# Flamingo block, two layers, one core: the way from the inputs to the first loop of maxima, reordered

## The reference, cut to what matters

```
x = x + tanh(g_xattn[0]) * attention0(layernorm(x), ctx, ctx)
x = x + tanh(g_ffn[0])   * experts0(layernorm(x))          # 8 experts, top 2, gelu
x = x + tanh(g_xattn[1]) * attention1(ctx, ctx, layernorm(x), mask)
x = x + tanh(g_ffn[1])   * experts1(layernorm(x))          # 8 experts, top 2, silu gate
attention: q = x Wq + bq; k = ctx Wk + bk; v = ctx Wv + bv
           out = softmax(q k^T / sqrt(8)) v, per head; then Wo, bo
```

## Time and profile before

| | us |
|---|---|
| median of 3 runs | 2752.51 (2747.73 to 2755.5) |
| the profiled execution | 2751.86 |
| its span | 2749.9 |
| PE busy | 2538.1 (92%) |
| DVE busy | 2161.0 (79%) |
| ACT busy | 1939.8 (71%) |
| POOL busy | 41.2 (1%) |
| mean granted TensorE clock | 0.942 |

### The profile page before, as it was taken

How to read it: one execution, slowest core, us unless ns; L and a number is a source line. 1 busy time by engine, 2 the same in 40 slices (tenths; PEclk the granted TensorE clock), 3 DMA queues, 4 the chain that set the end, 5 groups by cost and what they waited for, 6 DMA issues and landing times.

```text
span 2749.9 us, 55587 instructions
## 1 busy us (share of the span) xinstructions
PE 2538.1 (92%) x23426; PEld 1015.6 (37%) x23428; DVE 2161.0 (79%) x2210; ACT 1939.8 (71%) x3545; POOL 41.2 (1%) x28
## 2 busy tenths in 40 slices
PE   2389999999999999997893899999999999999979
PEld 1243333333333333344441333333333333333334
DVE  5479999999999999944434899999999999999235
ACT  2058888888888888874330288888888888888942
POOL 3000000000000000000010000000000000000000
PEclk8559999999999999998895699999999999999989
DMA  7120000000000000003101000000000000000010
GB/s 247 67 77 27 28 27 27 27 28 29 28 29 28 27 28 27 20 32 112 62 0 61 9 28 29 28 29 29 27 27 27 27 28 28 29 29 15 2 62 8
DMA packets 38627, 103.11 MB, mean 37 GB/s; under 512 B 4164, under 2 KB 14936, under 8 KB 38120
## 3 DMA queue, kind: packets, MB, share of 16 engines
q1 hardware_dynamic: 36936, 99.14, 9.8%
q10 hardware_dynamic: 1440, 0.40, 0.1%
HBM read 83.72 MB, written 15.80 MB: 36 GB/s over the span
## 4 chain that ended last, share of the span: by engine, by line
PE 67%; DVE 26%; DMA 3%; SPq 3%; issue 1%; ACT 1%; POOL 1%; DVEq 0%; ACTq 0%; POOLq 0%
DVE m_part L654 24%; PE ps L971 23%; PE ps L923 20%; PE ps L942 10%; PE ps L1069 4%; PE ps L1077 3%; PE ps L990 3%; SPq L294 2%; PE ps L883 1%; DMA q_parts<-probs 1%; PE ps L913 1%; SPq L303 1%; DMA probs<-in_mask_t 1%; PE ps L875 1%; DVE probs L610 1%
## 5 line engine op out<-in xcount | busy, mean ns | idle before, releaser
L654 DVE TENSOR_REDUCE m_part<-ps 128x2 f32<-128x1024 f32 (+1 forms) x1664 | 1933.9, 1183 | 239.3 <-PE ps L942 235.6
L492 ACT ACTIVATE probs<-ps 128x512 f32<-128x512 f32 (+1 forms) x3264 | 1763.8, 595 | 366.1 <-PE ps L923 254.1
L971 PE MATMUL ps<-probs,v_all 128*9 128x256 f32 x13056 | 1013.4, 382 | 1.5 <-ACT o_raw L472 0.5
L923 PE MATMUL ps<-q_ring,k_ring 35*128 35x512 f32 x3264 | 864.8, 498 | 0.6 <-ACT q_ring L481 0.4
L942 PE MATMUL ps<-k_ring,q_ring 33*128 33x512 f32 (+1 forms) x3328 | 726.8, 419 | 92.4 <-DVE m_part L654 36.2
L923 PEld LDWEIGHTS ps<-q_ring,k_ring 35*128 35x128 f32 x3264 | 343.1, 183 | 665.9 <-ACT probs L492 560.6
L942 PEld LDWEIGHTS ps<-k_ring,q_ring 33*128 33x128 f32 x3328 | 349.9, 194 | 175.3 <-DVE m_part L654 101.4
L971 PEld LDWEIGHTS ps<-probs,v_all 128*9 128x9 f32 x13056 | 194.1, 88 | 551.0 <-ACT probs L492 445.0
L990 PE MATMUL ps<-neg_i,zeros 128*9 128x256 bf16 x2664 | 115.3, 276 | 0.0
L675 DVE RECIPROCAL r_den<-ps 128x8 f32<-128x8 f32 x32 | 6.6, 207 | 121.4 <-PE ps L950 121.4
L789 DVE TENSOR_TENSOR probs<-probs,k_ring 128x512 f32<-128x512 f32 x64 | 43.6, 691 | 64.9 <-ACT probs L525 56.6
(11 more groups left out here) (121 smaller groups left out, 598.7 us busy)
## 6 DMA issues: line engine op xcount, KB each, us to landing
k_ring<-k_parts SPq DMA_DIRECT2D x384, 96.0 KB
k_ring<-k_parts SPq DMA_DIRECT2D x128, 112.2 KB
k_ring<-gate_rows SPq DMA_DIRECT2D x16, 512.0 KB, 7.4
probs<-in_mask_t SPq DMA_DIRECT2D x10, 640.0 KB, 4.5
k_parts<-probs SPq DMA_DIRECT2D x12, 512.0 KB, 3.1
k_parts<-big SPq DMA_DIRECT2D x12, 512.0 KB, 3.1
q_ring<-q_parts SPq DMA_DIRECT2D x128, 32.0 KB
big<-in_w SPq DMA_DIRECT2D x1, 2048.0 KB, 10.8
```

Of the source, the lines that this page charges most:

```text
L492: A(probs[0:k, n % PSLOTS, HALF * half:HALF * half + HALF], ps[0:k, e_bank(unit), :], ACT.Exp, scale=SCALE).then_inc(sem(f"exp_done{l}"), 1)
L654: V.tensor_reduce(m_part[:, h % 2, :, p, c], mx(n % 2)[:, :, 0:chunk_w[c]], AX.X, ALU.max).then_inc(sem(f"mx_done{l}"), 1)
L923: pe.matmul(bank, k_ring[row:row + ROWS_EXP, koff:koff + P], q_ring[row:row + ROWS_EXP, qoff:qoff + HALF], start=not masked, stop=True).th ...
L971: mm = pe.matmul(ps[32 * g:32 * g + VW, 7, 0:QGW], v_all[0:k, t, h, :], probs[0:k, n % PSLOTS, QGW * g:QGW * g + QGW], start=(t == 0), sto ...
```

## The change

- The ones come by DMA. GpSimd fills a small tile of 3 x 204 ones; SP writes the three rows of each half with one transfer that reads this tile 64 times over (`set_ones`). GpSimd's memsets of 32 rows go, in both layers. TensorE waits for the ones ahead of the first loop.
- Values are projected between keys: `values(0, c)` follows `keys(0, c)`, and ScalarE evacuates both in turn (`project_kv`). The first loop holds none.
- First keys group by group: SP stores three chunks, loads the queries of head 0, stores three more, loads group 0, stores three, loads group 1, and so on (`load_first0`). TensorE waits for all 13 splits ahead of the first loop, since the loop uses the same two banks.
- The mask is summed inside the heads: SP issues mask chunk h - 2 in its turn for head h, and ScalarE sums chunk h - 1 in step 12 of heads 1 to 11. The stage for it lies in another place (`sum_stage`).
- `total_mask` runs ahead of the key and value work of head 15.

```diff
+ONES_W = 204
+MASK_AT = 12
...
+        sum_stage = [spare[:, n * MCH * TQ // 4:(n + 1) * MCH * TQ // 4].bitcast(U8) for n in range(2)]
+        sum_junk = spare[:, 2 * MCH * TQ // 4:3 * MCH * TQ // 4].bitcast(BF16)
+        ones_at = ga_at + 6 * QT * E + 6 * QT
+        ones_w = spare[0:3, ones_at:ones_at + ONES_W]
-        RING_SET = 4 + 2 * KRING, 6 + 2 * KRING
+        RING_SET = 2 + 2 * KRING
+        ONES_IN = 2 * 16
...
-            def store_k(l):
-                for c in range(NCH):
+            def store_k(l, c0=0, c1=NCH):
+                for c in range(c0, c1):
                     sp.wait_ge(sem(f"k_split{l}"), c + 1)
                     sp.dma_start(k_parts[l][:, :, HALF * c:HALF * c + chunk_w[c]],
                                  k_st[l][:, c % KST, :, 0:chunk_w[c]].bitcast(F32)).then_inc(sem(f"k_stored{l}_{c % KST}"), 16)
+
+            def set_ones(l):
+
+                sp.wait_ge(sem("ones_w"), 1)
+                if l:
+                    sp.wait_ge(sem("gated0"), 2 * E * 4)
+                wide = KRING * KW
+                for row in (KR, HB + KR):
+                    sp.dma_start(k_ring[row:row + 3, 0:wide].bitcast(F32).rearrange("p (n w) -> p n w", w=ONES_W),
+                                 ones_w[:, :].rearrange("p (o w) -> p o w", o=1).broadcast_to([3, wide // ONES_W, ONES_W])
+                                 ).then_inc(sem("ones_in"), 16)
 
             def store_q(l):
                 for half in range(2):
                     sp.wait_ge(sem(f"q_split{l}"), half + 1)
                     sp.dma_start(q_parts[l][:, :, HALF * half:HALF * half + HALF], q_st[:, half, :, :].bitcast(F32)).then_inc(sem(f"q_stored{l}"), 16)
 
-            def check_mask():
-                for c in range(NFULL // MCH):
-                    if c > 1:
-                        sp.wait_ge(sem("mask_summed"), c - 1)
-                    sp.dma_start(mask_stage[c % 2].rearrange("p (t q) -> p t q", q=TQ),
+            def check_mask(c):
+                if c > 1:
+                    sp.wait_ge(sem("mask_summed"), c - 1)
+                if c == 0:
+                    sp.wait_ge(sem("q_proj0"), 2)
+                if c < NFULL // MCH:
+                    sp.dma_start(sum_stage[c % 2].rearrange("p (t q) -> p t q", q=TQ),
                                  a["mask_t"][c * MCH * P:(c + 1) * MCH * P, :].rearrange("(t p) q -> p t q", p=P)
                                  ).then_inc(sem(f"mask_in{c % 2}"), 16)
-                sp.wait_ge(sem("mask_summed"), NFULL // MCH - 1)
-                sp.dma_start(mask_stage[0][0:TAIL, 0:TQ], a["mask_t"][NFULL * P:TK, :]).then_inc(sem("mask_in0"), 16)
+                else:
+                    sp.dma_start(sum_stage[c % 2][0:TAIL, 0:TQ], a["mask_t"][NFULL * P:TK, :]).then_inc(sem(f"mask_in{c % 2}"), 16)
...
                 sp.wait_ge(sem("ffn_done0"), 1)
+                sp.wait_ge(sem("ones_in"), 2 * ONES_IN)
...
-            def ready(l, what):
+            def ready(l, what, c1=NCH):
 
                 if what == "q":
                     sp.wait_ge(sem(f"q_stored{l}"), 16 * 2)
                 else:
                     for n in range(KST):
-                        sp.wait_ge(sem(f"k_stored{l}_{n}"), 16 * len(range(n, NCH, KST)))
-
-            def load_first(l):
-
-                sp.wait_ge(sem("ring_set"), RING_SET[l])
-                ready(l, "k")
-                if l:
-                    for g in range(len(K_GROUPS)):
-                        load_keys(l, 0, g)
-                    store_q(l)
-                ready(l, "q")
-                load_queries(l, 0)
-                if l == 0:
-                    for g in range(len(K_GROUPS)):
-                        load_keys(l, 0, g)
-                load_queries(l, 1)
+                        sp.wait_ge(sem(f"k_stored{l}_{n}"), 16 * len(range(n, c1, KST)))
+
+            def load_first0():
+
+                sp.wait_ge(sem("ring_set"), RING_SET)
+                for g, (c0, c1) in enumerate(K_GROUPS):
+                    if g == 0:
+                        store_k(0, 0, c1)
+                        ready(0, "q")
+                        load_queries(0, 0)
+                    if g + 1 < len(K_GROUPS):
+                        store_k(0, *K_GROUPS[g + 1])
+                    ready(0, "k", c1)
+                    load_keys(0, 0, g)
+                load_queries(0, 1)
                 for g in range(len(K_GROUPS)):
-                    load_keys(l, 1, g)
-                load_queries(l, 2)
+                    load_keys(0, 1, g)
+                load_queries(0, 2)
+
+            def load_first1():
+
+                set_ones(1)
+                ready(1, "k")
+                for g in range(len(K_GROUPS)):
+                    load_keys(1, 0, g)
+                store_q(1)
+                ready(1, "q")
+                load_queries(1, 0)
+                load_queries(1, 1)
+                for g in range(len(K_GROUPS)):
+                    load_keys(1, 1, g)
+                load_queries(1, 2)
...
                 for h in range(KRING, H):
+                    if l == 0 and h - KRING <= NFULL // MCH:
+                        check_mask(h - KRING)
...
             setup()
+            set_ones(0)
             store_q(0)
-            store_k(0)
-            load_first(0)
-            check_mask()
+            load_first0()
             load_heads(0)
...
             spread_gates(0)
-            load_first(1)
+            load_first1()
...
-            def set_ring(l):
-
-                wide = E * TQ if l else KRING * KW
-                if l:
-                    pool.wait_ge(sem("gated0"), 2 * E * 4)
-                cleared = []
-                if l == 0:
-                    cleared += [k_ring[row:row + 32, off + TK:off + KW] for row in (0, HB) for off in range(0, KRING * KW, KW)]
-                    cleared += [q_ring[row:row + 32, :] for row in (KR, HB + KR)]
+            def set_ring():
+
+                nc.gpsimd.memset(ones_w[:, :], 1.0).then_inc(sem("ones_w"), 1)
+                pool.wait_ge(sem("ones_w"), 1)
+                cleared = [k_ring[row:row + 32, off + TK:off + KW] for row in (0, HB) for off in range(0, KRING * KW, KW)]
+                cleared += [q_ring[row:row + 32, :] for row in (KR, HB + KR)]
                 for n, part in enumerate(cleared):
                     nc.gpsimd.memset(part.bitcast(F32), 0.0).then_inc(sem("ring_set"), 1)
                     pool.wait_ge(sem("ring_set"), n + 1)
-                for n, row in enumerate((KR, HB + KR)):
-                    nc.gpsimd.memset(k_ring[row:row + 32, 0:wide].bitcast(F32), 1.0).then_inc(sem("ring_set"), 1)
-                    pool.wait_ge(sem("ring_set"), RING_SET[l] - 1 + n)
...
-                set_ring(0)
+                set_ring()
...
             constants()
-            set_ring(1)
...
-            def project_k():
-                for c in range(NCH):
-                    w = chunk_w[c]
-                    act.wait_ge(sem("k_proj0"), c + 1)
-                    if c >= KST:
-                        act.wait_ge(sem(f"k_stored0_{c % KST}"), 16 * (c // KST))
-                    A(k_st[0][:, c % KST, 0, 0:w], ps[:, c % 2, 0:w], ACT.Identity, bias=b_col[:, 0, 1:2]).then_inc(sem("k_evac0"), 1)
...
+            def project_kv():
+                for c in range(NCH):
+                    w = chunk_w[c]
+                    act.wait_ge(sem("k_proj0"), c + 1)
+                    if c >= KST:
+                        act.wait_ge(sem(f"k_stored0_{c % KST}"), 16 * (c // KST))
+                    A(k_st[0][:, c % KST, 0, 0:w], ps[:, c % 2, 0:w], ACT.Identity, bias=b_col[:, 0, 1:2]).then_inc(sem("k_evac0"), 1)
+                    set_v(c)
...
-                A(mask_junk[0:rows, 0:n], mask_stage[c % 2][0:rows, 0:2 * n].bitcast(U16), ACT.Copy,
+                A(sum_junk[0:rows, 0:n], sum_stage[c % 2][0:rows, 0:2 * n].bitcast(U16), ACT.Copy,
                   accum_out=m_sum[0:rows, c:c + 1]).then_inc(sem("mask_summed"), 1)
...
+                        if l == 0 and t == MASK_AT and 0 <= h - 1 <= NFULL // MCH:
+                            sum_mask(h - 1)
...
             project_q(0)
-            project_k()
-            for c in range(NCH):
-                set_v(c)
-                if c < NFULL // MCH + 1:
-                    sum_mask(c)
-            act.wait_ge(sem("mask_summed"), NFULL // MCH + 1)
+            project_kv()
             exp_all(0)
...
                 if l == 0:
+                    total_mask()
                     next_keys_values()
-                    total_mask()
...
                 with dve.If(dve.value_load(flag[0:1, 0:1], min_val=0, max_val=1) > 0):
+                    dve.wait_ge(sem("ones_in"), 2 * ONES_IN)
...
             def attention(l, masked):
+                pe.wait_ge(sem("ones_in"), ONES_IN * (l + 1))
+                pe.wait_ge(sem(f"k_split{l}"), NCH)
                 for i, unit in enumerate(FIRST_UNITS):
                     m_unit(l, unit, masked)
                     if i >= NU + 3:
```

(4 more changed lines are left out.)

## The result

The changed kernel takes **3119.18 us** (median of 4 runs, 3110.36 to 3127.17) against 2751.11 (4 runs, 2747.73 to 2755.5): the ratio is 1.1336, 95% interval 1.1294 to 1.1378. The forecast was 2719, its range 2698 to 2738. The profiled execution took 3125.63 us, its span is 3123.8 and its mean granted clock 0.798, against 0.942. Some executions of several kernels, the one before among them, take some 40 us longer at a lower mean clock; a ratio leaves out those over 1.5% above the fastest of their kernel.

A forecast was written before the change was run, and what follows sets the result against it. It held that two DMA engines carrying key loads set the start and three engines near their limit bound the heads. 2751.86 - 47.1 (front) + 21.4 (mask) - 7.0 (layer 1) plus 0.65: about 2719 us, range 2698 to 2738.

The forecast's parts named there:

- Mask inside the heads: Layer 0, heads 1 to 11: each sum holds ScalarE 2.34 us, TensorE stops behind it; +21.4 us, bounds 0 and 27.8.
- rival E: Heads 1 to 10, steps 13 to 20: TensorE's pause lowers its clock; with seven or eight slow steps about 2780; chance 0.07.
- Stretched VectorE groups: Layer 0 start: `var_e` and normalizing lose 19 us of excess; projections begin some 12 us earlier, which buys nothing.
- First loop at 75.0: Layer 0: the first loop starts at 75.0 instead of 71.3, after the last of 13 key chunks is split.
- the walk: Layer 0 start, transfers followed along the two key-load engines: weights land at 32.2, ones at 39.1, chunk 9 at 73.2.
- First loop of 72.5, values hidden, mask's hole gone: Layer 0's first loop drops 18.8 us of values and 31.9 of mask wait; front in sum -47.1 us.
- Ones in layer 1, -7.0: Before layer 1's first loop: two ones' transfers of 6.9 us replace 13.9 of memsets; bounds -12.6 to +6.8.
- Transfers in the heads at nothing: Layer 0's heads: the mask's transfers of 640 KB meet a DMA that is busy 8% and cost nothing.
- A: Layer 0 start: key loads don't hold up stores behind them; loop starts at about 60, 15 us less, 2704; chance 0.13.
- B: Layer 0's heads: the mask sum is hidden in ScalarE's idle time; 2698; chance 0.07.
- C: Both layers: the ones' transfers run on one engine, 13.8 us later in each layer; 2747; chance 0.08.
- D: Layer 0's heads: ScalarE reloads its function table around each sum, twice 1.3 us a head; about 2745; chance 0.05.

The follow-up runs named there:

- experiment 1: The changed kernel without the mask's transfers and sums, their result set to a constant: 2705.48 us, ratio 0.9813.
- experiment 4: The changed kernel with 80 small filler matmuls on TensorE at the end of step 13 of heads 1 to 10: 2729.35 us, ratio 0.9898.
- e4: The kernel before with only the mask's part of the change, transfers and sums inside the heads: 3152.98 us, ratio 1.143.
- e10: On e5 with key and query loads cut in two and long ones' packets: layer 0's expert weights issued later; 2657.45, 2657.61, 2700.07 and 2702.41 us.
- e5: The changed kernel with each mask sum cut into five pieces, in steps 2, 3, 4, 5 and 50 of a head: 2705.83 us, ratio 0.9817.
- e7: On e5: the ones' transfers use long packets, 6.5 KB rows in layer 0 and 16 KB in layer 1; 2701.6 us, ratio 0.9811.
- e8: On e5: each key or query load of 16 rows is cut into two of 8 rows; 2674.21 us, ratio 0.9723.
- e11: The changed kernel with the whole mask sum in step 2 of a head instead of 12: 2784.39, 2785.09, 2911.66 and 2941.71 us.
- e6_halves: The changed kernel with each mask sum in two halves of 1.27 us, in steps 12 and 30: 2734.62 us, ratio 0.9906.

## Why the prediction was wrong

**The step that failed** is the cost of "Mask inside the heads", +21.4 us: it is the pauses alone, with nothing for the clock behind them. The mask in the heads cost 414 us (experiment 1), 390 of them by the clock (experiment 4). The mechanism up to the pause was right: the sum stands behind the exps of step 12, TensorE stops within two scores and VectorE with it, and with the clock held up a head takes 69.23 us where 69.2 was forecast. The clock's fall was seen as rival E, but there its price and its chance were wrong. The price, "with seven or eight it is about **2780**", let the clock come back within eight steps. It stayed down for 307 us on end (242 to 549 us), with TensorE busy for all of them, and for 990 us in all, which is 414 us by the windows and not 61. The chance, 0.07, rested on "the pause is only 2 us and the engine is full on both sides of it". The pause was 1.58 us, and all six that met a full clock lowered it, as did all seven of `e4`. Why the clock stays down, and what of the filler brings it back, is open.

The warning stood in the trace of the kernel before. The earlier trace rows shows steps at 200 us at the low clock, and I read them as what the first loop leaves behind. They aren't: the clock had been at 1.00 again from 190 us on, and fell anew behind two short pauses in the first steps of head 0 (timeline and windows of the kernel before):
```profile
196.61 0.50 PE L942 MATMUL ps<-k_ring,q_ring 33*128 33x512 f32 x2 [0.38 <-DVE m_part L654]
197.74 0.50 PE L942 MATMUL ps<-k_ring,q_ring 33*128 33x512 f32 x2 [0.40 <-DVE m_part L654]
...
195.00:199.00 4.00, 3.22 (x34) 1.37 (x30) 3.67 (x4) 3.15 (x6) 0.00 (x0) 1.00 0.00 0
200.00:206.00 6.00, 6.00 (x58) 2.37 (x60) 2.80 (x3) 2.64 (x6) 0.00 (x0) 0.50 0.01 3
206.00:210.00 4.00, 4.00 (x52) 1.56 (x48) 3.41 (x4) 2.75 (x6) 0.00 (x0) 0.99 0.00 0
```
Two pauses of 0.4 us were followed by a fall, so "only 2 us" was no reason to trust a pause, though no run tests whether these two caused it. The clock was back at 206, in a step with filler, whereas behind step 12 the next filler is in step 47.

The Trainium skill ("TensorE: Matmul & The Clock Gate", part on the HAM clock gate) says that the clock has two levels and that sustained activity of the array releases the upper one. The two levels agree with the windows above (those in between mix the two); that sustained activity is enough does not, if it is read as a busy TensorE, by the 115.18 us at 0.50 with TensorE busy for all of them.

Point by point, the others:
- **Stretched VectorE groups:** right. `var_e` 0.17 us, the normalizing 2.14 at 8.22, and it buys nothing, since the stores stand behind the weights; `e10` shows the cover (12.7 us when it is taken away, "up to 12" in the prediction).
- **First loop at 75.0:** came at 79.13, 4.1 late, behind the split of the last chunk as said. The mis-sized term is the ones: by the trace's packets they passed from 30.9 to 43.2 us, in 12.3 us instead of 6.9, and so were done 4.1 us later than the walk's 39.1. From there to the loop it is 36.0 us, where the walk has 35.9 (and 36.1 in `e5`, 35.6 in `e7`). No run took the ones away or made them fast in layer 0, so this rests on the trace alone. The walk's last sum, 73.7 plus 1.0, is 74.7 and not 75.0. The key stores landed in 9.1 us, and SP was held in issuing from 16.21 to 33.11.
- **First loop of 72.5, values hidden, mask's hole gone:** right, 72.12 us. The front gave 43.3 us of 47.1.
- **Ones in layer 1, -7.0:** -1.5. The mis-sized term is the packet: the two transfers took 13 us where 6.9 were booked. With long packets (`e7`) it is 5.5 us less, and that gives the -7.0.
- **Transfers in the heads at nothing:** right (0.7 us).
- **Rivals:** A (loads don't hold stores) is false, by `e8`; B (sum hidden) is false for one sum at step 12 (experiment 4: 24 us remain) and true for pieces in the filler steps; C didn't occur (2.27 engines are more than one), nor D (the timeline has the exps right behind the accumulator's read, 0.09 us after it began). With the clock held up by filler the kernel takes 2729 us (experiment 4), inside the range; the rest of the sum is off by some 10 us, which are in the main the 3.8 of the front, the 5.5 of layer 1 and 2.5 in the heads.

The Trainium skill ("DMA: Bandwidth & Descriptors", part on how many engines a DMA uses) gives the number of engines by the slowest dimension, eight for a load of eight rows. `e8` was built on it, and the fall of the wait from 20.4 to 4.9 us agrees.

## What to carry to other kernels

Before a long instruction is put on the engine that feeds TensorE, work out the pause it makes on TensorE. In a kernel like this one count a pause of half a microsecond or more as a possible loss of the full clock for the rest of the stage, not as its own length. Cut such work into pieces that the buffers cover, or give TensorE independent filler in the hole, and put the pieces beside steps that have slack. Don't count on a busy TensorE to bring the clock back: here its steps without filler never did. And where a trace shows the low clock, look at what TensorE did just before it fell, not only at the stage before.

## What the runs showed of the hardware

- TensorE at 0.50 (1.2 GHz) can stay there while it is 100% busy: 115.18 us of a head, and 307 us on end. Pauses of 1.58 or 1.59 us were followed by its fall 13 times of 13 (the changed kernel and `e4`), those of 1.09 or 1.10 us six times of nine (`e11`), those of 0.50 to 0.52 us once of 19 (`e6_halves`), and with 80 small matmuls in the hole there was no fall (`e1`).
- In the changed kernel it came back six times, always in the steps with filler around a head's start or about 2 us behind them, and in four heads these steps didn't bring it back.
- One kernel's time spread by 157 us (2784 to 2942), its mean granted clock from 0.924 to 0.861 (`e11`).
- The ones' packets of 816 bytes, from SBUF to SBUF, took 13 us for 384 in layer 1, where at the 54 ns of the mask's 1 KB packets on three engines it would be 6.9. In packets of 16 KB (`e7`) the same rows took 7.2 us.
- A query store queued behind sixteen key loads on two engines waited 20.4 us; behind loads cut into 8 rows each it waited 4.9 (`e8`).
